# Two DMA transposes in place of one for the feed-forward's inner rows

## The chip, the cores and the metric

The kernel runs on one core of a Trainium2 chip. The metric is the device time of one launch in microseconds (us), as the median of the runs; lower is better. Before the change three runs took 2278.31, 2278.43 and 2281.01 us. TensorE is PE in the profile, its weight loads PEld, VectorE DVE, ScalarE ACT, GpSimd POOL, and SyncE SP; SPq is the queue on which SyncE issues transfers.

## The reference

What is computed is a transformer layer on x of 8 x 1024 x 512, float32: the rows are normalized, and windowed attention and a feed-forward are both added to x. The change touches the feed-forward alone:

```python
gate = fp4_linear(x, w_gate)      # x 8192 x 512, w_gate 1408 x 512
y = fp4_linear(x, w_up)
h = jax.nn.silu(gate) * y         # the inner rows, 8192 x 1408
return fp4_linear(h, w_down)      # w_down 512 x 1408
```

`fp4_linear` first rounds both operands in blocks of 16 along the last axis: each block is divided by its scale (the largest magnitude over 6), rounded to one of eight magnitudes, and multiplied by the scale again. Each of `gate`, `y` and the output row is then a plain product.

## The kernel before

The attention runs first and leaves its sum with x in device memory. The feed-forward follows, over 64 tiles of 128 rows, with `w_gate`, `w_up` and `w_down` resident in SBUF as fp16 pairs (a high part and a low part whose sum is the value). Each engine runs one `step` per tile in its own program. Four steps at the start and seven at the end are written out; the 56 between them are a loop of two steps each. Nothing but semaphores orders the engines against each other. `since` puts a wait on a semaphore's count, `hold` only increments a counter, and the list `held` has no other use.

One tile goes through these stages, and the names are those of the profile:

- PE multiplies the turned rows `turned` by the two weights in three column chunks into the PSUM banks `gu` (lines 1220 to 1225; 72 matmuls).
- ACT takes the silu into `sg`, and DVE multiplies it into `hv`, the inner rows in float32 (L1116).
- DVE works out block scales in `hs`, POOL divides by them (L164), ACT makes the rounding constants `hm` (L210), DVE rounds (L203, L205).
- POOL multiplies the whole 128 x 1408 tile by its scales (`value`, L169). ACT writes its fp16 high part to `hh[:, 0]` (`high`, L215, semaphore `h_high`), and POOL writes the rest to `hh[:, 1]` (`low`, L174, semaphore `h_low`).
- SP issues a DMA transpose of `hh` into `ht` (L1066): 22 blocks of 128 columns, 11 of the high part and 11 of the low part. `ht` has two buffers, by the tile's parity, with a semaphore each.
- PE's `down` (L1230 to L1238) multiplies `ht` by `w_down` into a PSUM bank `dn`: 11 pairs of matmuls with the high part's blocks (L1235 and L1237), then 11 matmuls with the low part's (L1235), 33 in all.
- DVE adds the attention's part and writes `fo` (L1134), and SP stores it.

PE works on `gu` of tile t in step t, and then on `down` of tile t-2. So the high and low parts of tile t-1 are made and turned during step t, while `down` needs them a step later. At the end there is no more `gu`: the last two `down` follow each other, of tiles 62 and 63.

SP's program for one step is, in order: the load of rows for tile t+3, the store of tile t-3 and the load of the attention's part, the transpose of `hh` of tile t-1, and the transpose of the input rows of tile t+2 (L1071, `turned<-split`, 8 blocks). ACT's `high` also waits until the transpose before it has landed (L1185).

Of the kernel before, what the change touches and what calls it, by code (L numbers as in the profile page):

```python
# [21 lines left out]
FC = FF // P  # L22
# [70 lines left out]
def hold(engine, passed):  # L93

    engine.sem_inc(passed, 1)
# [35 lines left out]
def since(engine, sem, count):  # L131

    if not isinstance(count, int) or count > 0:
        engine.wait_ge(sem, count)
# [73 lines left out]
def rounder(act, q, v, m, i):  # L208
    since(act, q["scaled"], i + 1)
    act.activation(m, v, ACT.Abs, scale=ROUND_Y).then_inc(q["rounder"], 1)  # L210


def high(act, q, v, h, i):
    since(act, q["valued"], i + 1)
    act.activation(h[:, 0], v, ACT.Copy).then_inc(q["high"], 1)  # L215
# [771 lines left out]
def feed_forward(nc, normed, part, late, wsc, rows, out):  # L987

    with ExitStack() as ctx:  # L989
        def sb(name, shape, dt=F32):  # L990
            return ctx.enter_context(nc.sbuf_tensor(name, shape, dt))

        def sem(name):
            return ctx.enter_context(nc.semaphore(name))
# [8 lines left out]
        hh = sb("hh", [P, 2, FF], F16)  # L1003
        ht = sb("ht", [P, 2, 2 * FC, P], F16)
# [7 lines left out]
        xq, x_in = rows.q, rows.x_in  # L1012
        p_in = [sem("p_in0"), sem("p_in1")]
        hq = {n: sem(f"h_{n}") for n in STAGES}
        xt_in, ht_in = [sem("xt_in0"), sem("xt_in1")], [sem("ht_in0"), sem("ht_in1")]
        gu_done, silu_done, h_done = sem("gu_done"), sem("silu_done"), sem("h_done")
        down_done, final = sem("down_done"), sem("ffn_final")
        stored = [sem("fstored0"), sem("fstored1")]
# [10 lines left out]
        def steps(engine, step):  # L1029
            for t in range(4):  # L1030
                step(t - t % 2, t % 2)
            with engine.Fori(2, NT // 2 - 2) as pair:
                for k in range(2):
                    step(pair * 2, k)
            for t in range(NT - 4, NT + DRAIN):
                step(t - t % 2, t % 2)

        def has(i, n):
            return not isinstance(i, int) or 0 <= i + n < NT

        held = [sem(f"fheld_{e}") for e in ("dve", "pe", "pool", "sp")]

        @block.sync
        def _(sp):
            for k in range(2):
                sp.dma_start(pr[:, k, :], part_t[k]).then_inc(p_in[k], 16)
            sp.wait_ge(xq["low"], 1)
            sp.dma_start(xr[:, 0, :], x_t[2]).then_inc(x_in[0], 16)

            def step(i, k):  # L1050
                t, o = i + k, 1 - k
                if has(i, k + 3):
                    since(sp, xq["low"], t + 2)
                    hold(sp, held[3])
                    sp.dma_start(xr[:, o, :], x_t[3:][t]).then_inc(x_in[o], 16)
                if has(i, k - 3):
                    since(sp, final, t - 2)
                    hold(sp, held[3])
                    sp.dma_start(out_t[i + (k - 3)], fo[:, o, :]).then_inc(stored[o], 16)
                    if has(i, k - 1):  # L1060
                        sp.dma_start(pr[:, o, :], part_t[i + (k - 1)]).then_inc(p_in[o], 16)
                if has(i, k - 1):
                    since(sp, hq["low"], t)
                    since(sp, down_done, t - 2)
                    hold(sp, held[3])
                    sp.dma_start_transpose(ht[:, o], hh[:, :, :].rearrange("p a c -> p (a c)")).then_inc(ht_in[o], 16)  # L1066
                if has(i, k + 2):
                    since(sp, xq["low"], t + 3)
                    since(sp, gu_done, t * 3 + 3)
                    hold(sp, held[3])  # L1070
                    sp.dma_start_transpose(xt[:, k].rearrange("p a n j -> p (a n) j"),  # L1071
                                           xh[:, :, :].rearrange("p a c -> p (a c)")).then_inc(xt_in[k], 16)

            steps(sp, step)
            for q in stored:
                sp.wait_ge(q, 16 * NT // 2)
# [3 lines left out]
        def part_of(n):  # L1080
            lo, size = PARTS[n]
            return slice(lo, lo + size), [hs[:, m, lo // QB:(lo + size) // QB] for m in range(4)]
# [86 lines left out]
        @block.scalar  # L1169
        def _(act):  # L1170
            def round_hidden(t, k, n):
                cols, _ = part_of(n)
                rounder(act, hq, hv[:, k, cols], hm[:, cols], t * 2 + n)

            def silu(t, k, f):
                n = CHUNKS[f][1]
                if f == 0:
                    since(act, xq["gains"], t + 1)
                since(act, gu_done, t * 3 + (f + 1))
                act.activation(sg[:, f, 0:n], acc[2 * f][:, 0:n], ACT.Silu, scale=xg[:, k, 3:4]).then_inc(silu_done, 1)  # L1180

            def step(i, k):
                t, o = i + k, 1 - k
                if has(i, k - 1):
                    since(act, ht_in[k], i * 8)  # L1185
                    high(act, hq, hv[:, o, :], hh, t - 1)
                if has(i, k):
                    silu(t, k, 0)
                    silu(t, k, 1)
                if has(i, k + 2):  # L1190
                    rounder(act, xq, xr[:, k, :], xm[:, :], t + 2)
                if has(i, k):
                    silu(t, k, 2)
                if has(i, k + 2):
                    if isinstance(i, int) and i + k == 0:
                        act.wait_ge(rows.x_turned[1], 16)
                    since(act, xt_in[o], (i + 2 * k) * 8)
                    high(act, xq, xr[:, k, :], xh, t + 2)
                if has(i, k):
                    round_hidden(t, k, 0)  # L1200
                    round_hidden(t, k, 1)

            steps(act, step)

        @block.tensor
        def _(pe):
            def gate_up(i, k, f):
                if f == 0:
                    if isinstance(i, int) and i == 0:
                        pe.wait_ge(rows.x_turned[k], 16)  # L1210
                    else:
                        since(pe, xt_in[k], i * 8)
                lo, n = CHUNKS[f]
                since(pe, h_done, (i + k) * 3 + (f - 2))
                g, w = (acc[m][:, 0:n].rearrange("p (r j) -> p r j", j=P) for m in (2 * f, 2 * f + 1))
                for c in range(KC):
                    x_hi, x_lo = xt[:, k, 0, c], xt[:, k, 1, c]
                    g_hi, g_lo = (late[:, lo // P:(lo + n) // P, a, c, :] for a in range(2))
                    u_hi, u_lo = (late[:, FC + lo // P:FC + (lo + n) // P, a, c, :] for a in range(2))
                    pe.matmul(g, x_hi, g_hi, start=(c == 0), stop=False)  # L1220
                    pe.matmul(g, x_hi, g_lo, start=False, stop=False)  # L1221
                    pe.matmul(w, x_hi, u_hi, start=(c == 0), stop=False)  # L1222
                    pe.matmul(w, x_hi, u_lo, start=False, stop=False)  # L1223
                    pe.matmul(g, x_lo, g_hi, start=False, stop=(c == KC - 1))  # L1224
                    last = pe.matmul(w, x_lo, u_hi, start=False, stop=(c == KC - 1))  # L1225
                last.then_inc(gu_done, 1)

            def down(i, k):

                since(pe, final, i + (k - 1))  # L1230
                since(pe, ht_in[k], i * 8 + 16)
                for at in range(2 * FC):
                    a, c = divmod(at, FC)
                    w_hi, w_lo = (late[:, 2 * FC + c, b].rearrange("p n j -> p (n j)") for b in range(2))
                    last = pe.matmul(dps[k][:, :], ht[:, k, at], w_hi, start=(at == 0), stop=(at == 2 * FC - 1))  # L1235
                    if a == 0:
                        pe.matmul(dps[k][:, :], ht[:, k, at], w_lo, start=False, stop=False)  # L1237
                last.then_inc(down_done, 1)  # L1238

            def step(i, k):  # L1240
                if has(i, k):
                    for f in range(3):
                        gate_up(i, k, f)
                if has(i, k - 2):
                    down(i - 2, k)

            steps(pe, step)
# [38 lines left out]
```

## Time and profile before

| | us |
|---|---|
| median of three runs | 2278.43 |
| the profiled execution, its own time | 2275.91 |
| its span, first to last instruction | 2274.1 |
| the feed-forward's first matmul starts at | 893.22 |
| one step of the feed-forward, repeated | 21.38 |
| PE busy over the span | 2160.4 |

Times in the rows count from the start of the span. A row of the timeline gives a start, a duration, the engine, the line and the tiles, and in brackets how long the engine had been idle and what released it. A row of a matmul lasts until its result is out, so rows of neighbouring matmuls overlap; the distance between their starts is what one of them costs. A row of SPq is the time in which the queue issues a transfer; the time from there to the landing is given separately. A granted clock of 1.00 is 2.4 GHz and 0.50 is 1.2 GHz.

### The profile page before, as it was taken

How to read it: one execution, taken by the hardware profiler on the slowest of the kernel's cores; microseconds unless marked ns; L12 is line 12 of the kernel's file. 1: busy time of each engine (PE TensorE's matmuls, PEld its weight loads, DVE VectorE, ACT ScalarE, POOL GpSimd, SP SyncE). 2: the span in 40 equal slices, each digit the busy share in tenths (PEclk: the TensorE clock that was granted, in tenths of full speed). 3: DMA queues.
4: the chain of work that ended last, by engine and by line, in shares of the span. 5: the costliest groups of instructions: out<-in, count | busy, mean ns of one | idle time of the engine just before them, and what ended most of it. 6: DMA issues, size and time to landing. Idle time of an engine off the chain costs nothing.

```text
span 2274.1 us, 46572 instructions
## 1 busy us (share of the span) xinstructions
PE 2160.4 (95%) x16704; PEld 1041.8 (46%) x16704; DVE 1638.1 (72%) x3097; ACT 655.9 (29%) x1007; POOL 1220.4 (54%) x880
## 2 busy tenths in 40 slices
PE   1899999999999987999999999999999999999998
PEld 0454444444444443444444444444444444444443
DVE  5587667666767555787787778778778777777774
ACT  1233334243333322222222222222222322222221
POOL 2166566566756444555555555555555555555552
PEclk9999999999999998999999999999999999999999
DMA  7547565664647427333333333433333333333332
GB/s 231 162 106 184 122 176 143 158 154 131 177 114 184 118 89 222 63 85 84 81 84 84 87 85 79 91 81 84 84 81 84 84 84 83 82 82 83 84 73 66
DMA packets 447373, 251.81 MB, mean 111 GB/s; under 512 B 365251, under 2 KB 371907, under 8 KB 447253
## 3 DMA queue, kind: packets, MB, share of 16 engines
q1 hardware_dynamic: 445860, 244.88, 43.9%
q10 hardware_dynamic: 1104, 4.19, 0.5%
q8 instruction: 99, 1.62, 0.3%
q0 software_dynamic: 288, 0.94, 0.1%
q14 instruction: 22, 0.17, 0.0%
HBM read 98.98 MB, written 59.77 MB: 70 GB/s over the span
## 4 chain that ended last, share of the span: by engine, by line
PE 59%; DVE 1%; POOL 0%; DMA 0%; issue 0%; POOLq 0%; ACT 0%; SPq 0%; DVEq 0%
PE dn L1235 13%; PE gu L1220 7%; PE gu L1224 7%; PE gu L1225 7%; PE gu L1222 7%; PE gu L1221 7%; PE gu L1223 7%; PE dn L1237 6%; POOL hv L169 0%; DMA ht<-hh 0%; DVE hv L205 0%; DVE hv L203 0%; POOLq L989 0%; DVE hv L1116 0%; DVE hs L179 0%
## 5 line engine op out<-in xcount | busy, mean ns | idle before, releaser
L904 PE MATMUL acc<-late 128*128 128x512 f16 x2304 | 527.8, 386 | 79.3 <-DMA late<-xh 56.0
L1235 PE MATMUL dn<-late,ht 128*128 128x512 f16 x1408 | 429.9, 380 | 5.3 <-DMA ht<-hh 5.3
L904 PEld LDWEIGHTS acc<-late 128*128 128x128 f16 x2304 | 221.4, 99 | 351.6 <-issue 99.7
L1116 DVE SCALAR_TENSOR_TENSOR hv<-gu,row_gains,sg 128x512 f32<-128x512 f32 (+1 forms) x192 | 129.0, 672 | 279.0 <-ACT sg L1180 279.0
L169 POOL TENSOR_TENSOR hv<-hv,hs 128x1408 f32<-128x1408 f32 x64 | 165.8, 2590 | 230.0 <-DVE hv L205 230.0
L1220 PE MATMUL gu<-late,turned 128*128 128x512 f16 (+1 forms) x768 | 277.9, 362 | 7.3 <-PEq L223 6.9
L1221 PE MATMUL gu<-late,turned 128*128 128x512 f16 (+1 forms) x768 | 277.8, 362 | 0.0
L1223 PE MATMUL gu<-late,turned 128*128 128x512 f16 (+1 forms) x768 | 277.8, 362 | 0.0
L1224 PE MATMUL gu<-late,turned 128*128 128x512 f16 (+1 forms) x768 | 277.8, 362 | 0.0
L1225 PE MATMUL gu<-late,turned 128*128 128x512 f16 (+1 forms) x768 | 277.8, 362 | 0.0
L1222 PE MATMUL gu<-late,turned 128*128 128x512 f16 (+1 forms) x768 | 277.8, 362 | 0.0
L1237 PE MATMUL dn<-late,ht 128*128 128x512 f16 x704 | 267.6, 380 | 0.0
L164 POOL TENSOR_TENSOR hv<-hv,hs 128x1024 f32<-128x1024 f32 (+1 forms) x128 | 177.5, 1387 | 111.2 <-DVE hs L185 111.2
L174 POOL TENSOR_TENSOR hh<-hv,hh 128x1408 f16<-128x1408 f32 x64 | 183.0, 2859 | 98.9 <-ACT hh L215 98.9
L1235 PEld LDWEIGHTS dn<-late,ht 128*128 128x128 f16 x1408 | 137.9, 98 | 169.0 <-issue 6.8
L215 ACT ACTIVATE hh<-hv 128x1408 f16<-128x1408 f32 x64 | 88.1, 1377 | 366.1 <-POOL hv L169 366.1
L904 PE MATMUL prj<-wo,oh 128*128 128x512 f16 x768 | 179.5, 384 | 10.5 <-DVE res L729 7.5
L210 ACT ACTIVATE hm<-hv 128x1024 f32<-128x1024 f32 (+1 forms) x128 | 101.2, 790 | 227.7 <-POOL hv L164 227.7
L1180 ACT ACTIVATE sg<-gu,row_gains 128x512 f32<-128x512 f32 (+1 forms) x192 | 119.9, 642 | 158.2 <-PE gu L1225 157.9
L169 POOL TENSOR_TENSOR raw<-raw,scales 128x512 f32<-128x512 f32 x64 | 67.8, 1059 | 141.9 <-DVE raw L205 141.9
L520 POOL TENSOR_TENSOR res<-res,bias 128x512 f32<-128x512 f32 x64 | 85.0, 1329 | 95.7 <-DMA res<-in_L_attn_x 95.6
L837 ACT ACTIVATE qk<-acc 128x512 f32<-128x512 f32 x128 | 75.4, 594 | 178.7 <-PE acc L904 176.7
(124 smaller groups left out, 3258.7 us busy)
## 6 DMA issues: line engine op xcount, KB each, us to landing
late<-in_L_attn_x SPq DMA_DIRECT2D x64, 256.0 KB, 3.6
normed<-late SPq DMA_DIRECT2D x64, 256.0 KB, 2.4
res<-in_L_attn_x SPq DMA_DIRECT2D x64, 256.0 KB, 2.9
attended<-res SPq DMA_DIRECT2D x64, 256.0 KB, 2.5
raw<-normed SPq DMA_DIRECT2D x64, 256.0 KB, 2.7
pr<-attended SPq DMA_DIRECT2D x64, 256.0 KB, 2.7
out<-fo SPq DMA_DIRECT2D x64, 256.0 KB, 2.0
ready<-turned SPq DMA_DIRECT2D x36, 256.0 KB, 2.3
```

The lines of the kernel that those rows point to most:

```text
L164: pool.tensor_tensor(blocks(v), blocks(v), spread(s[2]), ALU.mult).then_inc(q["scaled"], 1)
L169: pool.tensor_tensor(blocks(v), blocks(v), spread(s[3]), ALU.mult).then_inc(q["valued"], 1)
L174: pool.tensor_tensor(h[:, 1], v, h[:, 0], ALU.subtract).then_inc(q["low"], 1)
L904: last = pe.matmul(out, lhsT, rhs, start=(at == 0), stop=(at == n - 1))
L1220: pe.matmul(g, x_hi, g_hi, start=(c == 0), stop=False)
L1221: pe.matmul(g, x_hi, g_lo, start=False, stop=False)
L1222: pe.matmul(w, x_hi, u_hi, start=(c == 0), stop=False)
L1223: pe.matmul(w, x_hi, u_lo, start=False, stop=False)
L1224: pe.matmul(g, x_lo, g_hi, start=False, stop=(c == KC - 1))
L1225: last = pe.matmul(w, x_lo, u_hi, start=False, stop=(c == KC - 1))
L1235: last = pe.matmul(dps[k][:, :], ht[:, k, at], w_hi, start=(at == 0), stop=(at == 2 * FC - 1))
L1237: pe.matmul(dps[k][:, :], ht[:, k, at], w_lo, start=False, stop=False)
```

## The change

The one transpose of 22 blocks becomes two of 11 blocks. The first turns the high part and waits for `h_high` and for the buffer of `ht`; the second turns the low part and waits for `h_low`. Each has its own pair of semaphores. PE waits for the first before the first matmul of `down`, and for the second before matmul 23. ACT's `high` waits for both of the tile before. The list `held` becomes one semaphore.

```diff
-        xt_in, ht_in = [sem("xt_in0"), sem("xt_in1")], [sem("ht_in0"), sem("ht_in1")]
+        xt_in = [sem("xt_in0"), sem("xt_in1")]
+        ht_in = [[sem(f"ht_{part_}{k}") for k in range(2)] for part_ in ("hi", "lo")]
...
                 if has(i, k - 1):
+                    since(sp, hq["high"], t)
+                    since(sp, down_done, t - 2)
+                    hold(sp, held)
+                    sp.dma_start_transpose(ht[:, o, 0:FC], hh[:, 0, :]).then_inc(ht_in[0][o], 16)
                     since(sp, hq["low"], t)
-                    since(sp, down_done, t - 2)
-                    hold(sp, held[3])
-                    sp.dma_start_transpose(ht[:, o], hh[:, :, :].rearrange("p a c -> p (a c)")).then_inc(ht_in[o], 16)
+                    hold(sp, held)
+                    sp.dma_start_transpose(ht[:, o, FC:2 * FC], hh[:, 1, :]).then_inc(ht_in[1][o], 16)
...
                 if has(i, k - 1):
-                    since(act, ht_in[k], i * 8)
+                    for q in ht_in:
+                        since(act, q[k], i * 8)
                     high(act, hq, hv[:, o, :], hh, t - 1)
...
                 since(pe, final, i + (k - 1))
-                since(pe, ht_in[k], i * 8 + 16)
                 for at in range(2 * FC):
                     a, c = divmod(at, FC)
+                    if c == 0:
+                        since(pe, ht_in[a][k], i * 8 + 16)
```

The end of SP's program, from the last transpose of input rows on, stood like this; `h_low` is the semaphore of POOL's low part, `down_done` that of PE's `down`:

```order
L1071 DMA_TRANSPOSE turned<-split 128x8x128 [waits x_low,gu_done]
L1059 DMA out<-fo 128x512 [waits ffn_final]
L1061 DMA pr<-attended 128x512
L1066 DMA_TRANSPOSE ht<-hh 128x22x128 [waits h_low,down_done]
L1059 DMA out<-fo 128x512 [waits ffn_final]
```

And now:

```order
L1075 DMA_TRANSPOSE turned<-split 128x8x128 [waits x_low,gu_done]
L1060 DMA out<-fo 128x512 [waits ffn_final]
L1062 DMA pr<-attended 128x512
L1067 DMA_TRANSPOSE ht<-hh 128x11x128 [waits h_high,down_done]
L1070 DMA_TRANSPOSE ht<-hh 128x11x128 [waits h_low]
L1060 DMA out<-fo 128x512 [waits ffn_final]
```

One row became two of half the blocks, and the first of them waits for ACT's `h_high` instead of POOL's `h_low`. The same pair stands in every step.

On PE, the last `down` of the program before (tile 63; `ht_in1` is the landing of the odd buffer) begins and ends so:

```order
L1235 MATMUL dn<-late,ht 128x512 [waits ht_in1,ffn_final]
L1237 MATMUL dn<-late,ht 128x512
...
L1237 MATMUL dn<-late,ht 128x512
L1235 MATMUL dn<-late,ht 128x512 x11
L989 UNCONDITIONAL_BRANCH
```

And now:

```order
L1241 MATMUL dn<-late,ht 128x512 [waits ht_hi1,ffn_final]
L1243 MATMUL dn<-late,ht 128x512
...
L1243 MATMUL dn<-late,ht 128x512
L1241 MATMUL dn<-late,ht 128x512 [waits ht_lo1]
L1241 MATMUL dn<-late,ht 128x512 x10
L989 UNCONDITIONAL_BRANCH
```

The matmuls are the same 33 in the same order; the first now waits for the high part's landing alone, and a second wait stands at the first matmul of the low part.

## Rows read from the trace of the kernel before

**Rows 1.** The page: span, and busy time of each engine with its instructions.

```profile
span 2274.1 us, 46572 instructions
PE 2160.4 (95%) x16704; PEld 1041.8 (46%) x16704; DVE 1638.1 (72%) x3097; ACT 655.9 (29%) x1007; POOL 1220.4 (54%) x880
```

**Rows 2.** Waits of PE over the span: us in total, times, longest.

```profile
PE gu L1220 <- PEq L223: 6.9, 1, 6.9
PE dn L1235 <- DMA ht<-hh: 5.3, 1, 5.3
```

**Rows 3.** Busy time by stretch: stretch, length, engines, PE clock, DMA share, GB/s.

```profile
1200.00:2000.00 800.00, 800.00 (x3927) 384.14 (x3926) 620.11 (x1211) 223.51 (x303) 433.29 (x266) 1.00 0.37 84
```

**Rows 4.** Chain of waits, feed-forward, two successive steps: start, us, what.

```profile
1498.92 2.38 PE dn L1235 x11
1520.30 2.37 PE dn L1235 x11
```

**Rows 5.** Timeline of the program's end, 2249 to 2271 us.

```profile
2249.69 2.59 POOL L169 TENSOR_TENSOR hv<-hv,hs 128x1408 f32<-128x1408 f32 x1 [3.60 <-DVE hv L205]
...
2250.96 0.43 SPq L1061 DMA_DIRECT2D pr<-attended  x1
...
2252.38 1.38 ACT L215 ACTIVATE hh<-hv 128x1408 f16<-128x1408 f32 x1 [5.72 <-POOL hv L169]
...
2253.83 2.85 POOL L174 TENSOR_TENSOR hh<-hv,hh 128x1408 f16<-128x1408 f32 x1 [1.55 <-ACT hh L215]
...
2254.26 2.54 PE L1235 MATMUL dn<-late,ht 128*128 128x512 f16 x11
2256.79 3.29 SPq L1066 DMA_TRANSPOSE ht<-hh  x1
...
2262.10 0.58 PE L1235 MATMUL dn<-late,ht 128*128 128x512 f16 x1 [5.30 <-DMA ht<-hh]
...
2268.23 2.54 PE L1235 MATMUL dn<-late,ht 128*128 128x512 f16 x11
2270.81 0.75 DVE L1134 SCALAR_TENSOR_TENSOR fo<-dn,hk,pr 128x512 f32<-128x512 f32 x1 [13.22 <-PE dn L1235]
```

**Rows 6.** Tile `ht`, whole program: its transposes (22 blocks), and their landing.

```profile
L1066 SPq DMA_TRANSPOSE ht<-hh x64: 3222/3332/3757, 925.2 to 2256.8; - x64
...
DMA to landing us min/median/max: 5.1/5.2/5.4
```

**Rows 7.** Tile `turned`, 1200 to 2200 us: transposes of 8 blocks, and their landing.

```profile
L1071 SPq DMA_TRANSPOSE turned<-split x47: 1232/1232/1237, 1208.6 to 2182.7; - x47
...
DMA to landing us min/median/max: 3.0/3.1/4.0
```

**Rows 8.** Stretches at the end; the last columns are PE clock, DMA share, GB/s.

```profile
2259.00:2261.00 2.00, 0.00 (x0) 0.00 (x0) 0.00 (x0) 0.00 (x0) 0.00 (x0) 1.00 1.17 217
...
2262.10:2264.80 2.70, 2.70 (x7) 0.99 (x8) 0.00 (x0) 0.00 (x0) 0.00 (x0) 0.50 0.00 0
```

**Rows 9.** PE's timeline in the attention: same-width matmuls after idle times.

```profile
331.20 4.45 PE L904 MATMUL acc<-late 128*128 128x512 f16 x10 [2.65 <-issue]
...
868.56 2.75 PE L904 MATMUL prj<-wo,oh 128*128 128x512 f16 x12 [0.94 <-DVE res L729]
874.68 4.31 PE L904 MATMUL prj<-wo,oh 128*128 128x512 f16 x12 [2.59 <-DVE res L729]
```

**Rows 10.** Timeline inside one repeated step, with the first matmul of a `down`.

```profile
1511.14 1.38 ACT L215 ACTIVATE hh<-hv 128x1408 f16<-128x1408 f32 x1 [5.72 <-POOL hv L169]
...
1515.23 0.33 PE L1225 MATMUL gu<-late,turned 128*128 128x384 f16 x1
...
1515.39 0.38 PE L1235 MATMUL dn<-late,ht 128*128 128x512 f16 x1
...
1515.56 3.33 SPq L1066 DMA_TRANSPOSE ht<-hh  x1
```

**Rows 11.** SP's queue after that transpose.

```profile
1524.83 1.23 SPq L1071 DMA_TRANSPOSE turned<-split  x1
```

More of the change, by code:

```diff
@@ L1039, in has @@
             return not isinstance(i, int) or 0 <= i + n < NT
-        held = [sem(f"fheld_{e}") for e in ("dve", "pe", "pool", "sp")]
+        held = sem("fheld")
         @block.sync
@@ L1057, in step @@
                     since(sp, final, t - 2)
-                    hold(sp, held[3])
+                    hold(sp, held)
                     sp.dma_start(out_t[i + (k - 3)], fo[:, o, :]).then_inc(stored[o], 16)
@@ L1062, in step @@
                 if has(i, k - 1):
+                    since(sp, hq["high"], t)
+                    since(sp, down_done, t - 2)
+                    hold(sp, held)
+                    sp.dma_start_transpose(ht[:, o, 0:FC], hh[:, 0, :]).then_inc(ht_in[0][o], 16)
                     since(sp, hq["low"], t)
-                    since(sp, down_done, t - 2)
-                    hold(sp, held[3])
-                    sp.dma_start_transpose(ht[:, o], hh[:, :, :].rearrange("p a c -> p (a c)")).then_inc(ht_in[o], 16)
+                    hold(sp, held)
+                    sp.dma_start_transpose(ht[:, o, FC:2 * FC], hh[:, 1, :]).then_inc(ht_in[1][o], 16)
                 if has(i, k + 2):
@@ L1069, in step @@
                     since(sp, gu_done, t * 3 + 3)
-                    hold(sp, held[3])
+                    hold(sp, held)
                     sp.dma_start_transpose(xt[:, k].rearrange("p a n j -> p (a n) j"),
```

## The prediction

> **What bounds the kernel now.** I read the page first. PE is busy 2160.4 of 2274.1 us [rows 1], which alone doesn't say that PE is never kept waiting, so the second view is the list of PE's waits. In the feed-forward it has one entry of weight that names the tile of this change: 5.3 us, once, at the first matmul of a `down`, released by the transpose of `hh` [rows 2]. The other one, 6.9 us, is the passage from the attention to the feed-forward and no part of the change.
>
> Third, the busy time by stretch. Over 800 us of the middle PE is busy for 800.00 at full clock (1.00, which is 2.4 GHz) [rows 3]. The chain of waits repeats there every 1520.30 - 1498.92 = 21.38 us and stays on PE [rows 4]. Eleven matmuls of 512 columns follow each other in 2.37 us, so one costs 0.2158 us. In this stretch an earlier landing of `ht` is worth nothing.
>
> So the place to read is the end of the program, in the timeline [rows 5]. POOL's `value` of tile 63 ends at 2249.69 + 2.59 = 2252.28. ACT's high part ends at 2252.38 + 1.38 = 2253.76, POOL's low part at 2253.83 + 2.85 = 2256.68. The transpose is issued at 2256.79, 0.11 after its wait is met, and lands 5.2 us later [rows 6], at 2261.99; PE starts at 2262.10, again 0.11 after. PE had finished tile 62 at 2254.26 + 2.54 = 2256.80. The remaining 33 matmuls end at 2268.23 + 2.54 = 2270.77, and DVE and the last store follow. This chain is exposed from end to end.
>
> Those 33 matmuls take 2270.77 - 2262.10 = 8.67 us. At the spacing of 0.2158 they would take 32 x 0.2158 + 0.38 = 7.29. The missing 1.38 us is the clock: it was still at 1.00 from 2259 to 2261, while PE idled, and stood at 0.50 (1.2 GHz) during 2262.10 to 2264.80 [rows 8].
>
> **The change at the end of the program.** The order's rows show that nothing new stands in front of the high part's transpose on SP. SP's last instruction before it, the load of the attention's part, is issued by 2250.96 + 0.43 = 2251.39 [rows 5]. The buffer of `ht` was last read by the `down` of tile 61, which ended before tile 62's 33 matmuls began, that is near 2256.80 - 7.29 = 2249.5. So the high part's transpose waits for ACT only and is issued at 2253.76 + 0.11 = 2253.87, which is 2.92 us earlier than the whole one.
>
> No row shows a transpose of 11 blocks. The bounds are 8 blocks, issued in 1.23 us and landed in 3.1 [rows 7], and 22 blocks, issued in 3.33 and landed in 5.2 [rows 6]. On the line between them a block costs (5.2 - 3.1) / 14 = 0.15 us above a fixed 1.9, and 11 blocks land in 3.1 + 3 x 0.15 = 3.55. I take 3.55, since 11 is next to 8, and keep 3.1 and 5.2 as ends. The high part then lands at 2257.42, and PE starts at 2257.53, 4.57 us earlier than before.
>
> The low part's transpose is issued when the whole one was, at 2256.79: the first, with half the issue time, about 1.7 us, has left SP by 2255.6. It lands by the same line at 2260.34, and even with the whole one's 5.2 us at 2261.99. PE needs it after 22 matmuls, at 2257.53 + 22 x 0.2158 = 2262.28. So the second wait is met at either end of the bounds, narrowly at the late end, and PE runs all 33 through. What is late next is PE itself. The store of tile 62, which stands behind both transposes on SP, is off this path.
>
> PE's idle time shrinks from 5.30 to 2257.53 - 2256.80 = 0.73 us. In the attention a group of 12 matmuls after 0.94 us of idle time took 2.75 us, which is full rate (11 x 0.2158 + 0.38 = 2.75), while 12 after 2.59 us took 4.31, and 10 after 2.65 took 4.45 [rows 9]. The clock should therefore stay at 2.4 GHz, and the 1.38 us come back too.
>
> The sum is 4.57 + 1.38 = 5.95 us. With the landing's ends it is 6.40 (3.1 us) and, where 5.2 us holds, PE starts 2.92 earlier after 2.38 us of idle time, near the 2.59 of the row with the low clock, and only about 2.9 is left.
>
> A rule of the Trainium skill speaks against such a split. The trace gives the two transposes together 3.8 us of fixed part where one had 1.9. The page "DMA: Bandwidth & Descriptors", section Rules for kernel authors, advises coalescing many small transfers into one large one, and its section Anatomy of one DMA gives a fit (for another issuing path) of about 2.0 us plus bytes over 436 GB/s. By that fit the whole tile of 720,896 bytes would land in 3.65 us, where the trace has 5.2, so the measured rate is lower, though the fixed part agrees with the line. A half would land in 2.83, and by this estimate PE would be held by tile 62 alone, the gain would be 5.3 + 1.4 = 6.7 us, and the time 2271.7. The second fixed part costs time only where both transposes start together; here the first starts 2.92 us ahead.
>
> **The change in the repeated steps.** PE's price of a step is 21.38 us with no idle time, so whatever is moved matters only if it reaches PE. The halves of tile t-1 would be issued at about 1512.6 (1511.14 + 1.38 + 0.11) and 1515.56 [rows 10] and land by 1519.2. PE reads them a step later, after 1515.39 + 21.38 = 1536.8, and ACT's next `high`, which now waits for both, comes at 1511.14 + 21.38 = 1532.5. Margins of 13 us and more hide both. SP issues two times 1.7 us instead of 3.33 and its next instruction starts at 1524.83 [rows 11]. Behind the earlier wait on SP stands nothing else that was served before `h_low`. Without this cover a late `ht` would cost its lateness in every step.
>
> The new wait of PE at matmul 23 is the one edit without a row of its own. The nearest row is the first matmul of `down`, which already carries a wait: it starts 0.16 us after the matmul ahead of it [rows 10], the normal distance for one of 384 columns, so a met wait costs nothing within the 0.01 us of the view. I take 0. The other end is a bared weight load and lost overlap, priced below. A gain is excluded, as the 33 matmuls and their order stay.
>
> The removed semaphores cost and save nothing that any row shows.
>
> **The sum against the measurement.** The profiled execution took 2275.91 us, its span 2274.1; after the change I expect 2270.0 and 2268.2. The median of the runs is 2.52 above the profiled execution, 2278.43, and the step is a fixed one at the end, so 2278.43 - 5.95 = 2272.5.
>
> **Rivals.**
> - The clock falls although PE idles for 0.73 us only, because tile 63 starts just where it would have fallen. Then only 4.57 comes back: 2273.9, a gain of 0.20%. For it: it did fall at this place before. Against it: the 12 at full rate after 0.94 us. Chance 0.07.
> - The high part lands as late as the whole did (a late completion, or the low part's transpose, issued 0.6 us before the high one's landing, sharing the DMA engines, whose share there was 1.17 [rows 8]). Gain 2.9, 2275.5. Against it: 8 blocks land in 3.1 us, with little spread. Chance 0.07.
> - Slower: the wait in the middle of a sum stops PE's run-ahead in each of the 63 `down` that lie in the solid stretch. A bared load (1041.8 / 16704 = 0.06 us, [rows 1]) and the lost overlap of two matmuls (0.38 - 0.2158 = 0.16) make 0.22 us, 63 times 14.1, less 5.95: +8.1, 2286.6. It decides from 5.95 / 63 = 0.094 us per `down`. For it: in the loop the count waited for comes out of a register, twice per `down` now. Against it: the first matmul's wait shows no such gap. Chance 0.04.
> - Something elsewhere in the program moves by a few us, since all code behind the changed lines moves and the attention has idle times that end in "issue", of 2.65 us for example [rows 9]. Those are in code that comes first and stays, so I give this 0.08, at 2276 with either sign.
>
> **How the numbers follow.** The forecast has 0.74, its own range is 2271 to 2274: the landing's line and its short end, and about 1 us of scatter of the medians (the three runs span 2.7). The range for 8 in 10 reaches to 2270.5 at the low end and to 2276.0 at the high end, which takes in the first two rivals and leaves out the slower one. About 0.2% of 2278.43, 4.6 us, is what a measurement of this kernel can tell from no change. The forecast lies 1.4 us beyond that, so a tenth of its chance falls inside: 0.67 faster from it, 0.03 from the clock rival, 0.02 from the last, together 0.72. Slower gets 0.04 and 0.02 of the last, 0.06. The rest, 0.22, is the same.
>
> **What the profile after would show.** PE's entry for the wait on `ht` at 0.7 us instead of 5.3; a transpose of 11 blocks at 1.7 us of issue and 3.5 to landing; two of them at the end, 2.9 us apart; the clock at 1.00 throughout the last `down`, which takes 7.3 us; no idle time of PE at matmul 23; steps of 21.38 us. The forecast is wrong if the steps are longer by more than 0.09 us, if the high part lands more than 1.5 us later than said, or if the end is as forecast and another stretch has changed.

## The result and the profile after

The changed kernel took 2272.82 us (median of 10 runs) against 2278.12 us for the kernel before (10 runs). The ratio is 0.9974, 95% interval 0.9965 to 0.9984, so 5.9 us less, with 3.6 to 8.0 in the interval. The two medians differ by 5.3 us, and the means of the same runs by 5.9. The forecast was 2272.5 and 5.95 us less.

The profiled execution took 2273.06 us with a span of 2271.3. The answer to [rows 2] is the list of PE's waits:

```profile
PE gu L1225 <- PEq L223: 7.7, 1, 7.7
...
PE dn L1241 <- DMA ht<-hh: 0.7, 1, 0.7
```

The wait for `ht` is still there, once, at 0.7 us instead of 5.3. The timeline of the end, which answers to [rows 5]:

```profile
2252.82 2.59 POOL L169 TENSOR_TENSOR hv<-hv,hs 128x1408 f32<-128x1408 f32 x1 [3.60 <-DVE hv L205]
...
2255.52 1.38 ACT L215 ACTIVATE hh<-hv 128x1408 f16<-128x1408 f32 x1 [5.74 <-POOL hv L169]
...
2256.97 2.86 POOL L174 TENSOR_TENSOR hh<-hv,hh 128x1408 f16<-128x1408 f32 x1 [1.57 <-ACT hh L215]
2257.00 1.38 SPq L1067 DMA_TRANSPOSE ht<-hh  x1
...
2257.39 2.54 PE L1241 MATMUL dn<-late,ht 128*128 128x512 f16 x11
2259.92 1.26 SPq L1070 DMA_TRANSPOSE ht<-hh  x1
...
2260.62 0.38 PE L1241 MATMUL dn<-late,ht 128*128 128x512 f16 x1 [0.69 <-DMA ht<-hh]
```

Read it from ACT: its high part ends at 2256.90, and SP issues the first transpose at 2257.00, while POOL is still at the low part. PE is done with tile 62 at 2257.39 + 2.54 = 2259.93 and starts tile 63 at 2260.62. The view of tile `ht`, with its transposes, answers to [rows 6]:

```profile
L1067 SPq DMA_TRANSPOSE ht<-hh x64: 1269/1400/1422, 925.4 to 2257.0; - x64
L1070 SPq DMA_TRANSPOSE ht<-hh x64: 1263/1382/1407, 928.4 to 2259.9; - x64
...
DMA to landing us min/median/max: 3.5/3.5/4.9
```

Each half lands in 3.5 us. Busy time by stretch, with PE's clock in the third column from the right, in the middle (as in [rows 3]) and during the last `down` (as in [rows 8]):

```profile
1200.00:2000.00 800.00, 800.00 (x3928) 384.17 (x3927) 622.63 (x1216) 222.23 (x303) 433.87 (x266) 1.00 0.37 83
...
2260.60:2267.90 7.30, 7.28 (x33) 3.12 (x33) 0.12 (x1) 0.00 (x0) 0.00 (x0) 1.00 0.36 85
```

The middle is as full as it was. The 33 matmuls run at 1.00 and take 7.28 us instead of 8.67.

**Why the spans differ by 2.8 us only.** From the end of tile 62 on PE to the end of tile 63 it was 2270.77 - 2256.80 = 13.97 us before and is 2267.90 - 2259.93 = 7.97 after, 6.00 less. But this execution reached the feed-forward later. Its first matmul, and the last that runs at the low clock (0.63 us instead of 0.38):

```profile
895.07 0.58 PE L1225 MATMUL gu<-late,turned 128*128 128x512 f16 x1 [7.69 <-PEq L223]
...
900.14 0.63 PE L1225 MATMUL gu<-late,turned 128*128 128x512 f16 x1
```

That is 1.85 us later than the 893.22 of before. From this matmul to the end of tile 62 it took 1364.86 us, against 1363.58 before: 13 matmuls ran at the low clock here and 7 there, at 0.21 us each. So the span is 6.00 - 1.85 - 1.28 = 2.87 us shorter. In the 14 profiled executions of this study this first matmul starts anywhere between 890.5 and 898.3 us. The four kernels with whole transposes in the repeated steps lie between 893.1 and 895.2, amid the others. From there to the end of tile 62 every one of the 14 takes 1363.4 to 1365.0 us. One pair of spans says little about a change of 6 us; the place where it acts says much.

### The profile page after: what moved, and what is told of

The parts are those of the page before. It is cut to its first block, busy times and chain, and to the rows that moved or that the text cites. A ratio compares the mean times of both kernels' runs of the same rounds, so it can differ in the third digit from the quotient of the medians.

```text
span 2271.3 us, 46700 instructions
## 1 busy us (share of the span) xinstructions
PE 2162.2 (95%) x16704; PEld 1042.9 (46%) x16704; DVE 1638.5 (72%) x3097; ACT 655.4 (29%) x1007; POOL 1219.6 (54%) x880
## 4 chain that ended last, share of the span: by engine, by line
PE 59%; DVE 1%; POOL 0%; DMA 0%; ACT 0%; issue 0%; ACTq 0%; SPq 0%; DVEq 0%
PE dn L1241 13%; PE gu L1225 7%; PE gu L1230 7%; PE gu L1226 7%; PE gu L1228 7%; PE gu L1229 7%; PE gu L1227 7%; PE dn L1243 6%; POOL hv L169 0%; DVE hv L205 0%; DMA ht<-hh 0%; DVE hv L203 0%; DVE hv L1120 0%; DVE hs L179 0%; ACT sg L1184 0%
```

## The experiments

Below, "the end" of a kernel is the time from PE's last result of tile 62 to its last result of tile 63.

**Split for the last tile only.**

```diff
+                    if isinstance(i, int) and t == NT:
...
+                    else:
+                        since(sp, hq["low"], t)
+                        since(sp, down_done, t - 2)
+                        hold(sp, held)
+                        sp.dma_start_transpose(ht[:, o], hh[:, :, :].rearrange("p a c -> p (a c)")).then_inc(ht_in[0][o], 16)
```

The first branch holds the two transposes of the change, for tile 63; the second one transpose of 22 blocks, for tiles 0 to 62.

> The transpose is split for the last tile (63) alone; the other 63 tiles keep one transpose of 22 blocks and one wait of PE. Theory (the whole gain is made at the end of the program): the same gain as the full change, 6.0 us or a ratio of 0.9974, with 0.7 us of idle time of PE before the last down and the clock at 1.00 in it. Rival (the repeated steps gain or lose something): the gain differs from the full change's by more than 2 us, and the step differs from 21.38 us.

Ratio 0.9973, interval 0.9963 to 0.9983. PE waits 0.7 us and the end takes 7.95 us:

```profile
2257.20 1.27 SPq L1069 DMA_TRANSPOSE ht<-hh  x1
2260.12 1.39 SPq L1072 DMA_TRANSPOSE ht<-hh  x1
...
2260.83 0.38 PE L1249 MATMUL dn<-late,ht 128*128 128x512 f16 x1 [0.67 <-DMA ht<-hh]
```

One tile out of 64 makes the whole gain.

**Split for all but the last tile**, the same edit with the branches exchanged.

> The transpose is split for tiles 0 to 62 and whole for tile 63. Theory: no change against the kernel before, ratio 1.000 within 0.001, step 21.38 us, PE idle 5.3 us before the last down, which takes 8.7 us at the low clock at first. Rival (the second wait inside a down costs): up to 0.22 us in each of 62 steps, 14 us longer.

Ratio 1.0002, interval 0.9991 to 1.0012; PE's wait is 5.3 us, and the end takes 14.24 us. 63 pairs of transposes and 63 more waits of PE cost nothing that shows; by the interval they cost at most 2.7 us, 43 ns for each tile.

**Many waits**, on the kernel before.

```diff
-                since(pe, ht_in[k], i * 8 + 16)
                 for at in range(2 * FC):
                     a, c = divmod(at, FC)
+                    since(pe, ht_in[k], i * 8 + 16)
```

> The kernel before with one transpose, and PE's wait for it repeated before each of the 22 blocks of every down: 21 more waits in each of 64 downs, all of them met. Theory (a met wait costs PE nothing, since its sequencer runs ahead of matmuls of 0.216 us): step 21.38 us, ratio 1.000. Rival (a wait inside a sum stops the run-ahead): with 0.22 us for each wait in a down, 21 x 64 x 0.22 = 296 us longer, ratio 1.13; from 0.004 us per wait on it would be seen.

Ratio 1.0000, interval 0.9991 to 1.0008. The middle is as full as before, with the same 3927 matmuls in it:

```profile
1200.00:2000.00 800.00, 800.00 (x3927) 384.15 (x3926) 620.64 (x1214) 222.30 (x302) 432.50 (x266) 1.00 0.37 84
```

21 x 64 = 1344 more waits cost at most 1.8 us by the interval, 1.4 ns each. The slower rival is dead: it needed 94 ns. These waits are all on one semaphore; for a wait on a second one, as in the change, the bound is the 43 ns of the experiment before.

**Both halves issued after the low part.**

```diff
-                    since(sp, hq["high"], t)
+                    since(sp, hq["low"], t)
                     since(sp, down_done, t - 2)
                     hold(sp, held)
                     sp.dma_start_transpose(ht[:, o, 0:FC], hh[:, 0, :]).then_inc(ht_in[0][o], 16)
-                    since(sp, hq["low"], t)
                     hold(sp, held)
                     sp.dma_start_transpose(ht[:, o, FC:2 * FC], hh[:, 1, :]).then_inc(ht_in[1][o], 16)
```

> Two transposes and PE's two waits as in the change, but SP waits for the low part before it issues either, so the first isn't begun early. Theory: the high part lands at 2256.79 + 3.5, PE starts 1.7 us earlier than before after 3.6 us of idle time, the low part lands 1.4 us behind and is not waited for: gain 1.7 us, or 3.1 if the clock holds. Rival (begin early is worth nothing, the halved size is what counts): a gain of 6 us. Rival (two transposes back to back cost a second fixed part of 1.9 us on the path): PE waits at matmul 23.

Ratio 0.9991, interval 0.9981 to 1.0001, and 2275.98 us where the kernel before had 2277.45. The interval reaches 1, so the trace has to tell. PE starts after 3.74 us of idle time and isn't held at matmul 23. So halving alone brings PE's start forward by 5.30 - 3.74 = 1.56 us, and issuing the first half early by another 3.74 - 0.69 = 3.05: two thirds of the earlier start come from the early issue.

The view of tile `ht` shows what the second transpose costs when nothing keeps the two apart, first half and second half:

```profile
L1067 SPq DMA_TRANSPOSE ht<-hh x64: 1270/1400/1422, 927.7 to 2259.2; - x64
L1069 SPq DMA_TRANSPOSE ht<-hh x64: 1505/1598/1763, 929.2 to 2260.7; - x64
...
DMA to landing us min/median/max: 3.6/3.7/3.9
```

The second is issued 1.5 us after the first and lands 3.8 us after its own issue at the end of the program (the first 3.6). So all 22 blocks are there 5.3 us after the first issue, where the one transpose of 22 blocks takes 5.2. The two landings overlap, and the second fixed part is hardly paid at all, even before the 22 matmuls that would have hidden it.

In the timeline the clock does something new:

```profile
2262.97 0.38 PE L1240 MATMUL dn<-late,ht 128*128 128x512 f16 x1 [3.74 <-DMA ht<-hh]
...
2264.04 0.63 PE L1242 MATMUL dn<-late,ht 128*128 128x512 f16 x1
...
2267.45 0.38 PE L1242 MATMUL dn<-late,ht 128*128 128x512 f16 x1
```

The first five matmuls run at full rate; the low clock comes when PE has been busy again for 1.1 us, and lasts 3.4. The end takes 12.71 us.

The same kernel profiled once more:

> A second look at the kernel with both halves issued after the low part (idle 3.7 us), whose last down began at full clock and took 9.0 us. Theory (the cost of the low clock is a draw): another value, between 7.3 and 10.3 us, and the slow matmuls at other places of the down. Rival (fixed by the idle time): three fast matmuls first and 9.0 us again.

The end took 12.69 us, with four fast matmuls first (five before) and again eight slow ones. So this pair speaks for the rival, a cost fixed by the idle time.

**PE waits for both halves.**

```diff
-                    if c == 0:
-                        since(pe, ht_in[a][k], i * 8 + 16)
+                    if at == 0:
+                        for q in ht_in:
+                            since(pe, q[k], i * 8 + 16)
```

> Two transposes as in the change, the first begun at the high part, but PE waits for both before the first matmul of a down. Theory: the start of the last down follows the low part's landing, 2256.79 + 3.5 + 0.1 on the time axis of before, 1.7 us earlier than before, after 3.6 us of idle time. If the clock falls in that time: gain 1.7 us (0.9993); if it holds: 3.1 us (0.9986). Rival (the gain is made by the shorter transposes alone, not by PE's start on the high part): the gain is 6 us here too.

Ratio 1.0005, interval 0.9995 to 1.0015, less than either branch said. PE was 3.64 us idle and then found the low clock for 5.9 us, 14 matmuls, so that the `down` took 10.20 us and the end 13.84. The same kernel was profiled twice more, and timed again with the second of these:

> A second look at the kernel in which PE waits for both halves (idle 3.6 us). Its last down took 10.2 us in the first trace, longer than the 8.7 after 5.3 us of idle time. Theory (the low clock starts and ends at times that aren't tied to the down, so that its cost is a draw): another value here, between 7.3 and 10.3 us. Rival (the cost is fixed by the idle time): 10.2 again within 0.1.

> Timed once more, and a third look at its end. Its end (tile 62 done to tile 63 done on PE) took 13.8 us and 10.9 us in two traces against 14.0 to 14.7 with the whole transpose, while its first ratio was 1.0005, that is no gain. Theory (a gain of 0.1 to 3.7 us by the draw of the clock, some 1 to 2 us in the median): a ratio of 0.9990 to 0.9999. Rival (the wait of PE for both halves costs something elsewhere that eats the earlier landing): 1.0005 again, and a stretch of the trace other than the end that is longer than in the kernel before.

The last gave a ratio of 0.9992, interval 0.9980 to 1.0004, as the draw would have it. Neither timing comes near the 6 us of the first rival: what the change gains needs PE to start on the high part alone. The idle time was 3.64 us in all three traces. By stretch, the first trace has this during the first 14 matmuls of the last `down`:

```profile
2260.00:2265.80 5.80, 5.80 (x14) 1.94 (x14) 0.00 (x0) 0.00 (x0) 0.00 (x0) 0.50 0.00 0
```

and the second this during the whole of it:

```profile
2266.00:2273.20 7.20, 7.20 (x33) 3.10 (x33) 0.00 (x0) 0.00 (x0) 0.00 (x0) 1.00 0.00 0
```

In the second the clock didn't fall at all and the end took 10.92 us; in the third it took 12.61, with fast matmuls first. A cost fixed by the idle time is refuted here, though the pair of the experiment before had suggested it.

**PE kept busy, on the kernel before.** The 24 matmuls go to a bank that nobody reads any more.

```diff
+                if isinstance(i, int) and i + k == NT - 1:
+                    since(pe, h_done, NT * 3)
+                    for n in range(24):
+                        pe.matmul(acc[0][:, :].rearrange("p (r j) -> p r j", j=P), xt[:, k, 0, n % KC], late[:, 0:KC, 0, n % KC, :], start=True, stop=True)
                 since(pe, ht_in[k], i * 8 + 16)
```

> The kernel before, and PE fills its 5.3 us of idle time before the last down with 24 matmuls of 512 columns (24 x 0.2158 = 5.2 us) whose result nobody reads. The last down still starts when the whole transpose has landed, 5.3 us after the end of tile 62, but at a clock of 1.00. Theory (the gain has two terms, PE's earlier start of 4.6 us and the clock that doesn't fall): this kernel gains the second term alone, 1.4 us by the first trace and up to 2.1 by the other two kernels with a whole last transpose, a ratio of 0.9991 to 0.9994; from the end of tile 62 to the end of tile 63 it takes 5.3 + 7.3 = 12.6 us instead of 14.0 to 14.7. Rival (the low clock has another cause than the idle time): the down takes 8.7 us or more as before.

Ratio 0.9992, interval 0.9980 to 1.0003: as expected in size, though one timing can't tell it from nothing. The trace can:

```profile
2256.55 2.54 PE L1239 MATMUL dn<-late,ht 128*128 128x512 f16 x11
2258.92 5.34 PE L1234 MATMUL gu<-late,turned 128*128 128x512 f16 x24
...
2269.03 2.54 PE L1239 MATMUL dn<-late,ht 128*128 128x512 f16 x11
```

The end takes 2271.57 - 2259.09 = 12.48 us, all at full rate, while the transpose lands as late as before. The three kernels with a whole last transpose and idle PE took 13.97, 14.24 and 14.68. About 0.1 us of the difference isn't the clock: the busy PE began the `down` 5.2 us after the end of tile 62 and not 5.3. The `down` itself took 7.30 us where it took 8.67, 8.93 and 9.40, so the clock alone is worth 1.4 to 2.1 us.

**The last tile's high part in two column parts.** This is the version that the trace of the changed kernel points to: the remaining 0.7 us of idle time is the chain of `value`, `high` and the first transpose.

```diff
+                    if isinstance(i, int) and t == NT:
+                        for n, (lo, size) in enumerate(PARTS):
+                            s = [hs[:, m, lo // QB:(lo + size) // QB] for m in range(4)]
+                            value(pool, hq, hv[:, o, lo:lo + size], s, t - 1 + n, t * 2 - 1 + n)
...
+                        sp.dma_start_transpose(ht[:, o, 0:8], hh[:, 0, 0:1024]).then_inc(ht_in[0][o], 16)
+                        since(sp, hq["high"], t + 1)
+                        hold(sp, held)
+                        sp.dma_start_transpose(ht[:, o, 8:FC], hh[:, 0, 1024:FF]).then_inc(ht_tail, 16)
```

The first lines are POOL's; ACT's `high` is divided likewise, and the rest is SP's.

> The change, and for the last tile alone POOL's value and ACT's high part work on columns 0 to 1023 and then 1024 to 1407, the first as soon as the first part is rounded, and the high part is turned by two transposes of 8 and 3 blocks. Theory (the last 0.7 us of PE's idle time is the chain value, high, transpose of the high part): the 8 blocks land in 3.1 us, before PE ends tile 62, PE has no idle time at the end, and the time is 0.7 us below the full change's, a ratio of 0.9971 against before, which only the trace can tell from 0.9974. Rival: the added small transpose (3 blocks, by the line 2.4 us to landing) delays the low part's by its fixed part, and PE waits at matmul 17 or 23.

Ratio 0.9965, interval 0.9954 to 0.9975, median 2269.72 us.

```profile
2254.61 1.24 SPq L1069 DMA_TRANSPOSE ht<-hh  x1
2255.95 1.19 SPq L1072 DMA_TRANSPOSE ht<-hh  x1
2257.40 1.39 SPq L1077 DMA_TRANSPOSE ht<-hh  x1
...
2258.53 0.75 DVE L1151 SCALAR_TENSOR_TENSOR fo<-dn,hk,pr 128x512 f32<-128x512 f32 x1 [4.69 <-PE dn L1260]
2265.65 0.75 DVE L1151 SCALAR_TENSOR_TENSOR fo<-dn,hk,pr 128x512 f32<-128x512 f32 x1 [6.37 <-PE dn L1260]
```

The view of tile `ht` gives the shortest landing, that of the 3 blocks, first:

```profile
DMA to landing us min/median/max: 2.3/3.5/4.5
```

PE's list has no wait for `ht` left, and DVE's two last `fo` start 7.12 us apart, which is 33 matmuls at 0.2158. The first transpose is issued before PE is done with tile 62. The 8 blocks landed in 3.3 us rather than the expected 3.1, still in time. This kernel was timed again, and the change was timed beside its first timing, on the same chip:

> The kernel with the last tile's value and high part in two column parts once more, for its distance to the change. Theory: between 0.7 us (PE's idle time gone) and 1 us below the change: from the end of tile 62 to the end of tile 63 PE takes 7.1 us where the change takes 8.0, and the ratio against before is 0.997, with 0.9965 inside its interval. Rival (its first ratio, 0.9965, is a real 2 us more than the change's): 0.9965 again, and a stretch of the trace other than the end that is shorter.

> The full change again, beside the two others on the same chip. Theory: 5.95 us or ratio 0.9974, all of it between the end of tile 62 on PE and the end of tile 63; what differs before the repeated steps (the span of the kernel after was only 2.8 us shorter in its profiled execution, with the repeated steps beginning 3.1 us later) is scatter between executions and takes another value here. Rival (the change delays the passage from the attention to the feed-forward): the first matmul of the feed-forward is again at 895 us rather than 893.

The parts gave 0.9965 again (interval 0.9952 to 0.9979), with an end of 7.12 us in the trace; the change gave 0.9973 (0.9964 to 0.9983), with an end of 7.98 us. The change's feed-forward began at 893.12 us this time, so it doesn't delay the passage. That the parts are better is shown by the trace, 0.86 us at the end. The two ratios suggest 1.8 us, but each lies inside the other's interval, and the medians of the parts and of the change timed beside them, 2269.72 and 2270.42 us, differ by 0.7. No stretch accounts for more: from the feed-forward's first matmul to the end of tile 62 the parts take 1363.77 and 1363.66 us and this run of the change 1363.75.

## Why the prediction was right

- **What bounds the kernel.** Right: the repeated steps gave nothing (ratio 1.0002 with 63 of 64 tiles split), and the last tile alone gave everything.
- **The early start, 4.57 us.** The landing of 11 blocks was taken as 3.55 us from a line between 8 and 22 blocks and was 3.5. The idle time was forecast at 0.73 us and was 0.69. 5.30 - 0.69 = 4.61. The issue was off: 1.4 us instead of 1.7, with no effect. Of the two estimates for this landing the trace decides against the one by the fit of "DMA: Bandwidth & Descriptors" in the Trainium skill (section Anatomy of one DMA, for another issuing path), which would have given 2.83.
- **The coalescing rule against the split.** Here the prediction was right in the result and wrong in the reason. It said that the second fixed part costs time where both transposes start together. Each half by itself does take 3.5 us against 5.2 for the whole, but issued back to back they overlap, and both are there after 5.3 us. The rule as cited is about many small transfers, and each half is still 360,448 bytes.
- **The clock, 1.38 us.** Right in kind, since the last `down` took 7.28 us against a forecast of 7.29, and the kernel with busy PE shows this term by itself. Its size was read from one execution. Kernels whose PE idles for 5.3 us there took 8.67, 8.93 and 9.40 us for this `down`, so the term is 1.4 to 2.1 us, 1.7 in the mean, and the sum is nearer to 6.3 than to 5.95. The timings, 5.9 and 6.1, can't tell these apart: the first has an interval of 3.6 to 8.0. That the forecast was met to within 0.1 us is luck on top of a sound account.
- **The new wait inside `down`, 0.** Right, at most 1.4 ns for each met wait.
- **The rival in which the clock falls** after 0.7 us of idle time didn't occur in any of three traces (the change twice, the last tile alone once). The rival of the late landing didn't either. The last rival, something elsewhere, is the scatter ahead of the feed-forward, and has no sign that goes with a kernel. Why the low clock after 3.64 us of idle time came early, late or not at all stays open; no run here settles it.

## What to carry over

When an engine is full through a long loop, read what is left of a transfer's latency in the program's last iteration: there it stands open, with every producer ahead of it, and cutting the transfer along the order in which the consumer reads it pays once. Issue each piece as soon as its own producer is done, and look up in a trace whether the pieces' fixed costs add up or overlap before counting them. Price a gap of TensorE with the clock that it costs afterwards, from several executions, since one gives only a draw.

## What the runs showed of the hardware

- The low clock after a gap isn't fixed by the gap. After 3.64 us of idle time it cost 2.9, 0.0 and 1.7 us in three executions of one kernel (a `down` of 10.20, 7.28 and 8.97 us), and it can come more than 1 us after PE is busy again.
- DMA transposes land near a straight line in their blocks, 2.3, 3.1, 3.5 and 5.2 us for 3, 8, 11 and 22 of them, but their issue doesn't follow one: 1.19, 1.24, 1.4 and 3.3 us.
- Two DMA transposes of 11 blocks, issued 1.5 us apart on one queue, both land within 5.3 us of the first issue, against 5.2 us for one of 22 blocks. That is the kernel with both halves issued after the low part. The price is small: the first lands in 3.6 us instead of 3.5, and the second takes 1.5 to 1.8 us to issue instead of 1.4.
